# Switched attention in a fused eight-stage kernel: the context product over whole rows and one unit later, with the work of ScalarE, VectorE and GpSimd re-ordered around it

## The chip, the cores and the metric

One NeuronCore of one Trainium2 chip. The metric is the device time of one execution in microseconds (us); lower is better. The kernel before takes 3280.29 us (median of three runs, 3280.03 to 3283.74).

## What is computed

Eight residual sublayers, one after another, on x of shape 128 x 64 x 128: four attention or retention sublayers over a context and four feed-forward ones. The last one, `_L3_ffn_ref`, is the one that the change touches, "switched" attention. Cut to what matters:

```python
gate_v = _get_sel_gate(x, sel_v_w, rs)
gate_o = _get_sel_gate(x, sel_o_w, rs)
q = jnp.einsum('bsd,hpd->bhsp', x, q_w.reshape(H, P, D))
k = jnp.einsum('bsd,hpd->bhsp', x, k_w.reshape(H, P, D))
xv = jnp.einsum('bsd,hedp->bshep', x, v_w.reshape(H, E, D, P))
v = jnp.einsum('bshep,bshe->bhsp', xv, gate_v)
att = jax.nn.softmax(jnp.einsum('bhqp,bhkp->bhqk', q, k) * SCALE, axis=-1)
ctx = jnp.einsum('bhqk,bhkp->bqhp', att, v)
weighted = ctx[:, :, :, None, :] * gate_o[..., None]
out = jnp.einsum('bshep,hepd->bsd', weighted, o_w.reshape(H, E, P, D))
```

There are 8 heads, 8 experts per head, and P = D = 128. `_get_sel_gate` takes a sigmoid of the routing logits, keeps the best two of each head's eight experts, scales them to sum 1 and returns zeros for the others. The input x of the sublayer is first normalised (layer norm), and the result is added to x with a gate.

## The kernel before, in words

The function `switch_attention` is the last stage of the program. It works on 64 tiles. A tile is two batch elements of 64 rows, so 128 rows lie on the 128 partitions. All weights stay in SBUF, each split into a high and a low part, so that one product of high precision is three TensorE passes (high x high, low x high, high x low).

Per tile there are 16 **units**: eight value units v0 to v7 and eight output units o0 to o7, one for each head. A unit (`unit`, L2173) is six matmuls of 512 columns: three into a PSUM bank `ps_sw_a` for experts 4 to 7, then three into a bank `ps_sw_d` for experts 0 to 3. ScalarE empties the first bank (`scale`, L1914): four activations that multiply each expert's block by its gate and write it to `sw_scaled`. VectorE empties the second (`mix`, L2069): two steps of two `scalar_tensor_tensor` that multiply by the gate and accumulate in `sw_v_part` or `sw_o_part`. GpSimd adds up what both left (`add_v`, L1841 and L1846; `add_o`, L1860 to L1870; `finish`). There are two banks of each kind, so a unit may write its banks only when ScalarE and VectorE have emptied those of the unit two before.

Between the units stand the small steps of the tile. On TensorE: `turn_x` (transpose of the normalised x), `turn_probs`, `logits`, two `pair_keys` (L2206, products of 128 x 128, 4 in each), `scores` (L2230) and `context` (L2219, probabilities x values). On ScalarE: copies out of PSUM (`keep_x`, `keep_probs` L1931, `keep_u`, `keep_ctx` L1954) and four steps `exp_scores` (L1963), each the exponential of two heads with a read of the accumulated sum. On VectorE: 20 routing steps R0 to R19 (`route`, from `sw_r_plus` L2078 to `sw_gate_v` L2099), three parts of the layer norm's moments (`front`: `sw_stats`, `sw_mv`, `sw_var`), the normalisation itself (`norm`, `sw_xhat` L244), the row maxima of the scores (`peak`, L2124), the shift derived from them (`shifts`, L2130), the sums of the softmax, and the low parts of the context (`low_ctx`, L2118). On GpSimd: `rstd` (L236), a power of one column.

The order of the work is written out by hand: one list of (lag, step) for each engine, and `straight` issues, for every turn t and every entry in the order of the list, that step for tile t - lag. Each engine executes its list strictly in that order; semaphores tie the engines together. So in one turn TensorE works on the value units of tile t-2, the output units of tile t-3, the scores of tile t-1 and the context of tile t-2. The exponentials of tile t-1 (`exp_scores`) wait for `sw_shift` of the same turn. The text calls a stretch from one v0 to the next "a turn".

The context before is one product for each head and each batch element, on half of the rows:

```python
for h in range(SH):
    for b in range(2):
        t = slice(b * S, (b + 1) * S)
        m = pe.matmul(ps_w[b][:, h * S:(h + 1) * S], v[t, h], probs_T[t, h], start=True, stop=True)
```

Of the kernel before, what the change touches and what calls it, by code (L numbers as in the profile page):

```python
# [1682 lines left out]
def switch_attention(k, A, C, x_in, out):  # L1683
# [6 lines left out]
    with k.scope():  # L1690
# [84 lines left out]
        with nc.Block() as block:  # L1775
# [211 lines left out]
            def _(dve):  # L1987
                dve.memset(zeros[:], 0.0).then_inc(q["zeros"], 1)
                dve.wait_ge(q["zeros"], 1)
# [83 lines left out]
                def route(n):  # L2073


                    def step(i, s, rd):
# [4 lines left out]
                            lambda: dve.tensor_tensor(r["eq1"][:], r["p"][:], wide(rm["m1"][:]), ALU.is_equal),  # L2081
                            lambda: dve.tensor_tensor(r["w1"][:], r["eq1"][:], place[:], ALU.mult),
                            lambda: dve.tensor_reduce(rm["w1"][:], r["w1"][:], AX.X, ALU.max),
                            lambda: dve.tensor_tensor(r["sel1"][:], r["w1"][:], wide(rm["w1"][:]), ALU.is_equal),
# [210 lines left out]
```

## Time and profile before

| what | value |
|---|---|
| median of three runs | 3280.29 us (3280.03 to 3283.74) |
| the profiled execution: its own time | 3283.84 us |
| its span in the profile | 3282.1 us, 78570 instructions |
| TensorE matmuls busy | 2945.8 us (90%) |
| VectorE busy | 2780.9 us (85%) |
| ScalarE busy | 2342.4 us (71%) |
| GpSimd busy | 2319.9 us (71%) |
| chain that ended last | TensorE 57%, of it `ps_sw_a` L2173 23%, `ps_sw_d` L2173 21%, the context L2219 4% |

The span is cut by the profile page into 40 equal slices. The last 23 or so, from about 1400 us on, are the switched attention; there TensorE's digit is 9 (8 in the last slice) and the granted TensorE clock is 9 as well. The stages before it are not touched by the change. In a timeline row, the numbers are start and duration in us, then engine, line, operation and tiles; a value in brackets at its end is the idle time of that engine before it, with what released it. Consecutive instructions of ScalarE and VectorE overlap in their durations, so what one of them costs its engine is the distance to the next start.

### The profile page before, as it was taken

What the parts mean: (1) busy time and instruction counts of PE and PEld (TensorE: products, weight loads), DVE (VectorE), ACT (ScalarE), POOL (GpSimd) and SP (SyncE); (2) the same over time, 40 slices, a digit from 0 to 9 for tenths busy, and PEclk for the clock granted to TensorE, in tenths of its full rate; (3) what the DMA queues carried; (4) which work ended last, traced back from release to release, by engine and by line L of the source; (5) the groups of instructions that cost most, each with busy time, mean ns of one, the idle gap of its engine ahead of it and who ended that gap; (6) DMA issues with size and microseconds to landing.
All of it is one profiled execution on the core that took longest, in us unless ns stands there. A gap on an engine that the chain in (4) does not pass through costs nothing.

```text
span 3282.1 us, 78570 instructions
## 1 busy us (share of the span) xinstructions
PE 2945.8 (90%) x24633; PEld 2215.6 (68%) x24646; DVE 2780.9 (85%) x9101; ACT 2342.4 (71%) x7540; POOL 2319.9 (71%) x3111
## 2 busy tenths in 40 slices
PE   6639998289667999599999999999999999999998
PEld 5526775167435777477777777777777777777776
DVE  4369997599898998698898989898999889898987
ACT  3275665878796666477777777777777777777776
POOL 1179997565687666377777777777777777777777
PEclk7559998589678999799999999999999999999999
DMA  3000000022000110300000000000000000000000
GB/s 107 19 10 17 16 17 8 17 74 72 5 1 17 29 31 28 114 21 8 7 9 9 7 8 8 9 8 8 7 9 9 8 7 9 9 8 8 8 8 5
DMA packets 133086, 63.73 MB, mean 19 GB/s; under 512 B 20544, under 2 KB 132288, under 8 KB 132672
## 3 DMA queue, kind: packets, MB, share of 16 engines
q1 hardware_dynamic: 132672, 58.70, 6.3%
q8 instruction: 200, 3.28, 0.4%
q14 instruction: 214, 1.75, 0.2%
HBM read 41.82 MB, written 8.45 MB: 15 GB/s over the span
## 4 chain that ended last, share of the span: by engine, by line
PE 57%; ACT 1%; DVE 1%; POOL 0%; DMA 0%; issue 0%; SPq 0%; POOLq 0%; ACTq 0%; DVEq 0%
PE ps_sw_a L2173 23%; PE ps_sw_d L2173 21%; PE ps_sw_w L2219 4%; PE ps_sw_w L2206 3%; PE ps_sw_s L2188 2%; PE ps_sw_s L2230 2%; PE ps_sw_m L2195 1%; ACT sw_scaled L1914 0%; PE ps_sw_m L2181 0%; DVE sw_v_part L2069 0%; DMA sw_v<-in_L_ffn_v_w 0%; ACT sw_probs L1963 0%; DVE sw_v_low L2008 0%; ACT sw_v_high L1969 0%; PE ps_sw_w L2236 0%
## 5 line engine op out<-in xcount | busy, mean ns | idle before, releaser
L1914 ACT ACTIVATE sw_scaled<-ps_sw_a,sw_gate_o 128x128 f32<-128x128 f32 x2048 | 620.3, 447 | 254.1 <-PE ps_sw_a L2173 248.2
L1914 ACT ACTIVATE sw_scaled<-ps_sw_a,sw_gate_v 128x128 f32<-128x128 f32 x2048 | 597.4, 448 | 194.4 <-PE ps_sw_a L2173 192.7
L2069 DVE SCALAR_TENSOR_TENSOR sw_o_part<-ps_sw_d,sw_gate_o,sw_o_part 128x128 f32<-128x128 f32 x1920 | 554.9, 338 | 63.2 <-PE ps_sw_d L2173 60.5
L1841 POOL TENSOR_TENSOR sw_v_pair<-sw_v_part,sw_scaled 128x256 f32<-128x256 f32 x512 | 382.1, 746 | 156.0 <-DVE sw_v_part L2069 98.9
L2069 DVE SCALAR_TENSOR_TENSOR sw_v_part<-ps_sw_d,sw_gate_v,sw_scaled 128x128 f32<-128x128 f32 x1024 | 303.7, 337 | 122.1 <-PE ps_sw_d L2173 104.7
L1867 POOL TENSOR_TENSOR sw_o_rest<-sw_o_rest,sw_scaled 128x256 f32<-128x256 f32 x384 | 285.4, 743 | 157.9 <-ACT sw_scaled L1914 120.8
L2069 DVE SCALAR_TENSOR_TENSOR sw_v_part<-ps_sw_d,sw_gate_v,sw_v_part 128x128 f32<-128x128 f32 x1024 | 304.1, 337 | 0.0
L1870 POOL TENSOR_TENSOR sw_o_rest<-sw_o_rest,sw_scaled 128x256 f32<-128x256 f32 x384 | 282.6, 736 | 30.1
L1846 POOL TENSOR_TENSOR sw_v<-sw_v_pair 128x128 f32<-128x128 f32 x512 | 243.8, 476 | 40.1
L985 POOL TENSOR_TENSOR at_key_wide<-at_keyT,c_half_heads 128x1024 f32<-128x1024 f32 x128 | 242.6, 1895 | 4.2 <-ACT at_keyT L1082 4.2
L2173 PE MATMUL ps_sw_a<-sw_v_high,sw_xT_high 128*128 128x512 f32 x512 | 234.6, 458 | 8.2 <-DVE sw_v_low L2008 8.2
L2173 PE MATMUL ps_sw_a<-sw_o_high,sw_ctx_high 128*128 128x512 f32 x512 | 215.7, 421 | 0.5 <-ACT sw_scaled L1914 0.5
L2173 PE MATMUL ps_sw_d<-sw_v_high,sw_xT_high 128*128 128x512 f32 x512 | 207.2, 405 | 0.4 <-DVE sw_v_part L2069 0.4
L2173 PE MATMUL ps_sw_d<-sw_o_high,sw_ctx_high 128*128 128x512 f32 x512 | 202.2, 395 | 1.2 <-DVE sw_v_part L2069 1.2
L2173 PE MATMUL ps_sw_a<-sw_o_high,sw_ctx_low 128*128 128x512 f32 x512 | 203.0, 396 | 0.0
L2173 PE MATMUL ps_sw_d<-sw_o_low,sw_ctx_high 128*128 128x512 f32 x512 | 202.7, 396 | 0.0
L2173 PE MATMUL ps_sw_a<-sw_v_high,sw_xT_low 128*128 128x512 f32 x512 | 202.4, 395 | 0.0
L2173 PE MATMUL ps_sw_d<-sw_o_high,sw_ctx_low 128*128 128x512 f32 x512 | 202.2, 395 | 0.0
L2173 PE MATMUL ps_sw_a<-sw_o_low,sw_ctx_high 128*128 128x512 f32 x512 | 202.1, 395 | 0.0
L2173 PE MATMUL ps_sw_a<-sw_v_low,sw_xT_high 128*128 128x512 f32 x512 | 201.9, 394 | 0.0
L2173 PE MATMUL ps_sw_d<-sw_v_high,sw_xT_low 128*128 128x512 f32 x512 | 201.5, 394 | 0.0
L2173 PE MATMUL ps_sw_d<-sw_v_low,sw_xT_high 128*128 128x512 f32 x512 | 200.7, 392 | 0.0
(337 smaller groups left out, 8584.4 us busy)
## 6 DMA issues: line engine op xcount, KB each, us to landing
at_ctxT<-ctx_T SPq DMA_DIRECT2D x128, 64.0 KB, 1.8
re_values<-in_ctx SPq DMA_DIRECT2D x128, 64.0 KB, 2.4
x<-in_x SPq DMA_DIRECT2D x16, 256.0 KB, 3.4
l_ctx<-in_ctx SPq DMA_DIRECT2D x16, 256.0 KB, 3.0
re_ctx<-in_ctx SPq DMA_DIRECT2D x16, 256.0 KB, 3.2
scratch_x<-x SPq DMA_DIRECT2D x64, 64.0 KB, 1.9
sw_x<-scratch_x SPq DMA_DIRECT2D x64, 64.0 KB, 1.9
sw_x_res<-scratch_x SPq DMA_DIRECT2D x64, 64.0 KB, 1.8
```

Of the source, the lines that this page charges most:

```text
L985: pool.tensor_tensor(key_wide[:, s], keyT[:, s].unsqueeze(1).broadcast_to([P, HALF, P]), C["half_heads"][:].unsqueeze(2).broadcast_to([P, ...
L1841: pool.tensor_tensor(v_pair[:, h % 2], v_part[:, h], scaled[:, h % 4, 2:4], ALU.add)\
L1846: pool.tensor_tensor(v[:, h], v_pair[:, h % 2, 0], v_pair[:, h % 2, 1], ALU.add).then_inc(q["v"], 1)
L1867: pool.tensor_tensor(o_rest[:, 0:2], o_rest[:, 0:2], scaled[:, h % 4, 0:2], ALU.add)\
L1870: pool.tensor_tensor(o_rest[:, 2:4], o_rest[:, 2:4], scaled[:, h % 4, 2:4], ALU.add)\
L1914: act.activation(scaled[:, h % 4, e], ps_a[h % 2][:, e], ACT.Copy, scale=gates[:, s, h, HALF_E + e:HALF_E + e + 1]).then_inc(a_scaled[kind ...
L2069: dve.scalar_tensor_tensor(out=acc[:, e % 2], in0=ps_d[h % 2][:, e], scalar=gates[:, s, h, e:e + 1], in1=before, op0=ALU.mult, op1=ALU.add ...
L2173: m = pe.matmul(bank, lhs[a], w[b][:, h, experts], start=c == 0, stop=c == 2)
L2188: m = pe.matmul(ps_s[t, h], probs[t, s, h], C["ident"][t, t], start=True, stop=True)
L2206: m = pe.matmul(ps_w[n][:, h * P:(h + 1) * P], W["pair"][:, 4 * n + h], xT[:, s], start=True, stop=True)
L2219: m = pe.matmul(ps_w[b][:, h * S:(h + 1) * S], v[t, h], probs_T[t, h], start=True, stop=True)
L2230: m = pe.matmul(ps_s[t], xT[:, s, t], uT[:, :, t], start=True, stop=True)
```

## The change

Five things change, all in `switch_attention`:

- **Context.** `probs_T` becomes 128 x 8 x 128 with zeros outside two diagonal blocks of 64 x 64, cleared once by a memset. `keep_probs` writes the two blocks with two activations instead of one. `context` is then one product of 128 x 128 for each head (8 instead of 16), and it stands behind o2 instead of o1. PSUM bank 0 holds heads 0 to 3, bank 1 heads 4 to 7, each finished separately.
- **ScalarE's list.** Before, after o2: ctx 0, o3, exp 0, o4, ctx 1, o5, exp 1, o6, exp 2, o7, exp 3. Now, after o2: exp 0, exp 1, o3, ctx 0, o4, ctx 1, exp 2, o5, exp 3, o6, o7.
- **VectorE's list.** The norm moves from the head of the value half (for tile t-1) to the middle of the output half (for tile t, behind o2). The three `front` steps move from the output half to the value half. The first `low_ctx` comes one unit later; the second keeps its place. R19 moves one unit ahead.
- **GpSimd's list.** `rstd` moves from between o5 and o6 to directly behind the value units.
- **Scratch.** The tiles `eq1`/`eq2` and `w1`/`w2` of the routing are merged.

```diff
-        probs_T = k.sb("sw_probs_T", [P, SH, S])
+        probs_T = k.sb("sw_probs_T", [P, SH, P])
...
-                stages += [(3, add_o(h)) for h in range(6)] + [(0, rstd)] + [(3, add_o(h)) for h in range(6, SH)]
+                stages += [(0, rstd)] + [(3, add_o(h)) for h in range(SH)]
...
-                    act.activation(probs_T[:], ps_s, ACT.Copy).then_inc(q["p_kept"], 1)
+                    for b in range(2):
+                        t = slice(b * S, (b + 1) * S)
+                        act.activation(probs_T[t, :, t], ps_s[t], ACT.Copy).then_inc(q["p_kept"], 1)
...
-                stages += [(1, keep_u(0)), vs[6], (1, keep_u(1)), vs[7]] + os[:3] + [(2, keep_ctx(0)), os[3], exps[0]]
-                stages += [os[4], (2, keep_ctx(1)), os[5], exps[1], os[6], exps[2], os[7], exps[3]]
+                stages += [(1, keep_u(0)), vs[6], (1, keep_u(1)), vs[7]] + os[:3] + [exps[0], exps[1], os[3], (2, keep_ctx(0))]
+                stages += [os[4], (2, keep_ctx(1)), exps[2], os[5], exps[3], os[6], os[7]]
...
+                dve.memset(probs_T[:], 0.0).then_inc(q["zeros"], 1)
...
-                    "v": [[], [], [(2, sums(0))], [(2, sums(1))], [(2, sums(2))], [], *R[0:5], R[5] + R[6], R[7],
-                          R[8] + R[9], R[10], R[11]],
-                    "o": [R[12], R[13] + R[14], R[15] + R[16], [(1, peak)], [(1, shifts)], R[17], R[18],
-                          [(2, low_ctx(0))], [(0, front(0))], R[19] + [(0, front(1))], [(0, front(2))],
-                          [(2, low_ctx(1))], [], [], [], []],
+                    "v": [[], [], [(2, sums(0))], [(2, sums(1))], [(2, sums(2))], [(0, front(0))], *R[0:4],
+                          R[4] + [(0, front(1))], R[5] + R[6], R[7] + [(0, front(2))], R[8] + R[9], R[10], R[11]],
+                    "o": [R[12], R[13] + R[14], R[15] + R[16], [(1, peak)], [(1, shifts)], [(0, norm)] + R[17], R[18], R[19],
+                          [], [(2, low_ctx(0))], [], [(2, low_ctx(1))], [], [], [], []],
                 }
-                stages = [(1, norm), (1, only_first(keep_pairs))]
+                stages = [(1, only_first(keep_pairs))]
...
                     for h in range(SH):
-                        for b in range(2):
-                            t = slice(b * S, (b + 1) * S)
-                            m = pe.matmul(ps_w[b][:, h * S:(h + 1) * S], v[t, h], probs_T[t, h], start=True, stop=True)
-                            if h == SH - 1:
-                                m.then_inc(q["ctx"], 1)
+                        m = pe.matmul(ps_w[h // 4][:, h % 4 * P:(h % 4 + 1) * P], v[:, h], probs_T[:, h], start=True, stop=True)
+                        if h % 4 == 3:
+                            m.then_inc(q["ctx"], 1)
...
-                stages += [vs[5], (1, pair_keys(1)), vs[6], vs[7], os[0], (1, scores), os[1], (2, context)]
-                stages += os[2:]
+                stages += [vs[5], (1, pair_keys(1)), vs[6], vs[7], os[0], (1, scores), *os[1:3], (2, context)]
+                stages += os[3:]
```

How the lists come out on two engines. ScalarE in the output half of one turn, from the three `scale` steps of o0 to o2 on (x12), before:

```order
L1914 ACTIVATE sw_scaled<-ps_sw_a,sw_gate_o 128x128 x12
L1954 ACTIVATE sw_ctx_high<-ps_sw_w 128x8x64
L1914 ACTIVATE sw_scaled<-ps_sw_a,sw_gate_o 128x128 x4
L1963 ACTIVATE sw_probs,sw_total<-ps_sw_s,sw_shift 128x64 x2
L1914 ACTIVATE sw_scaled<-ps_sw_a,sw_gate_o 128x128 x4
L1954 ACTIVATE sw_ctx_high<-ps_sw_w 128x8x64
L1914 ACTIVATE sw_scaled<-ps_sw_a,sw_gate_o 128x128 x4
L1963 ACTIVATE sw_probs,sw_total<-ps_sw_s,sw_shift 128x64 x2
L1914 ACTIVATE sw_scaled<-ps_sw_a,sw_gate_o 128x128 x4
L1963 ACTIVATE sw_probs,sw_total<-ps_sw_s,sw_shift 128x64 x2
L1914 ACTIVATE sw_scaled<-ps_sw_a,sw_gate_o 128x128 x4
L1963 ACTIVATE sw_probs,sw_total<-ps_sw_s,sw_shift 128x64 x2
```

and now:

```order
L1914 ACTIVATE sw_scaled<-ps_sw_a,sw_gate_o 128x128 x12
L1967 ACTIVATE sw_probs,sw_total<-ps_sw_s,sw_shift 128x64 x4
L1914 ACTIVATE sw_scaled<-ps_sw_a,sw_gate_o 128x128 x4
L1958 ACTIVATE sw_ctx_high<-ps_sw_w 128x512
L1914 ACTIVATE sw_scaled<-ps_sw_a,sw_gate_o 128x128 x4
L1958 ACTIVATE sw_ctx_high<-ps_sw_w 128x512
L1967 ACTIVATE sw_probs,sw_total<-ps_sw_s,sw_shift 128x64 x2
L1914 ACTIVATE sw_scaled<-ps_sw_a,sw_gate_o 128x128 x4
L1967 ACTIVATE sw_probs,sw_total<-ps_sw_s,sw_shift 128x64 x2
L1914 ACTIVATE sw_scaled<-ps_sw_a,sw_gate_o 128x128 x8
```

The exponentials of four heads (x4) now stand ahead of o3, and all eight heads' stand ahead of o6.

VectorE around the shift, from the second mix of o1 on, before:

```order
L2069 SCALAR_TENSOR_TENSOR sw_o_part<-ps_sw_d,sw_gate_o,sw_o_part 128x128 x2
L2124 TENSOR_REDUCE sw_top<-ps_sw_s 128x8
L2069 SCALAR_TENSOR_TENSOR sw_o_part<-ps_sw_d,sw_gate_o,sw_o_part 128x128 x2
L2130 TENSOR_SCALAR sw_shift<-sw_top 128x8
L2069 SCALAR_TENSOR_TENSOR sw_o_part<-ps_sw_d,sw_gate_o,sw_o_part 128x128 x2
L2096 RECIPROCAL sw_m_inv<-sw_m_clip 128x16
```

and now:

```order
L2074 SCALAR_TENSOR_TENSOR sw_o_part<-ps_sw_d,sw_gate_o,sw_o_part 128x128 x2
L2131 TENSOR_REDUCE sw_top<-ps_sw_s 128x8
L2074 SCALAR_TENSOR_TENSOR sw_o_part<-ps_sw_d,sw_gate_o,sw_o_part 128x128 x2
L2137 TENSOR_SCALAR sw_shift<-sw_top 128x8
L2074 SCALAR_TENSOR_TENSOR sw_o_part<-ps_sw_d,sw_gate_o,sw_o_part 128x128 x2
L244 TENSOR_SCALAR sw_xhat<-sw_x,sw_mv,sw_rstd 128x128
L2101 RECIPROCAL sw_m_inv<-sw_m_clip 128x16
```

The maxima and the shift keep their places in VectorE's list; the norm (L244) comes in behind them.

## Rows read from the trace of the kernel before

**Rows 1.** Stretches: length, busy us of PE, PEld, DVE, ACT, POOL, then granted clock, DMA share, GB/s.
```profile
2000.00:2400.00 400.00, 400.00 (x2471) 306.68 (x2470) 359.85 (x1285) 303.66 (x1184) 303.68 (x470) 1.00 0.03 8
```
**Rows 2.** One line's instructions, 1420 to 3200 us: duration ns min/median/max, first and last start us.
```profile
L2124 DVE TENSOR_REDUCE sw_top<-ps_sw_s x60: 676/678/682, 1447.3 to 3194.7; 128x8 f32<-128x512 f32 x60
L2094 DVE TENSOR_TENSOR sw_m_sum<-sw_m_m x60: 268/490/511, 1446.2 to 3193.6; 128x16 f32<-128x16 f32 x60
```
**Rows 3.** Timeline of TensorE over one turn.
```profile
2432.99 0.47 PE L2173 MATMUL ps_sw_a<-sw_v_high,sw_xT_high 128*128 128x512 f32 x1
...
2433.76 0.48 PE L2173 MATMUL ps_sw_d<-sw_v_high,sw_xT_high 128*128 128x512 f32 x1
...
2442.07 1.05 PE L2206 MATMUL ps_sw_w<-sw_xT,sw_pair 128*128 128x128 f32 x8
2442.88 0.48 PE L2173 MATMUL ps_sw_a<-sw_v_high,sw_xT_high 128*128 128x512 f32 x1
...
2450.48 0.50 PE L2173 MATMUL ps_sw_a<-sw_o_high,sw_ctx_high 128*128 128x512 f32 x1
...
2452.07 2.00 PE L2219 MATMUL ps_sw_w<-sw_probs_T,sw_v 64*128 64x64 f32 x32
2454.00 0.50 PE L2173 MATMUL ps_sw_a<-sw_o_high,sw_ctx_high 128*128 128x512 f32 x1
...
2455.51 0.40 PE L2173 MATMUL ps_sw_a<-sw_o_high,sw_ctx_high 128*128 128x512 f32 x1
...
2462.57 0.47 PE L2173 MATMUL ps_sw_a<-sw_v_high,sw_xT_high 128*128 128x512 f32 x1
```
**Rows 4.** Timeline of VectorE in the same turn.
```profile
2446.19 0.80 DVE L2084 TENSOR_TENSOR sw_r_sel<-sw_r_w,sw_m_w 128x128 f32<-128x128 f32 x1
...
2451.98 0.27 DVE L2092 TENSOR_TENSOR sw_r_sel<-sw_r_sel 128x128 f32<-128x128 f32 x1
...
2453.01 0.49 DVE L2094 TENSOR_TENSOR sw_m_sum<-sw_m_m 128x16 f32<-128x16 f32 x1
...
2454.14 0.68 DVE L2124 TENSOR_REDUCE sw_top<-ps_sw_s 128x8 f32<-128x512 f32 x1
2455.71 0.61 DVE L2069 SCALAR_TENSOR_TENSOR sw_o_part<-ps_sw_d,sw_gate_o,sw_o_part 128x128 f32<-128x128 f32 x2 [0.89 <-PE ps_sw_d L2173]
2456.23 0.16 DVE L2130 TENSOR_SCALAR sw_shift<-sw_top 128x8 f32<-128x8 f32 x1
...
2460.39 0.17 DVE L220 BATCH_NORM_AGGREGATE sw_mv<-sw_stats 128x2 f32<-128x6 f32 x1
2460.49 0.57 DVE L2069 SCALAR_TENSOR_TENSOR sw_o_part<-ps_sw_d,sw_gate_o,sw_o_part 128x128 f32<-128x128 f32 x2
```
**Rows 5.** Timeline of VectorE at the stage's start, before GpSimd's adds begin.
```profile
1347.15 0.29 DVE L2084 TENSOR_TENSOR sw_r_sel<-sw_r_w,sw_m_w 128x128 f32<-128x128 f32 x1
```
**Rows 6.** Timeline of ScalarE in the same turn.
```profile
2443.86 1.14 ACT L1914 ACTIVATE sw_scaled<-ps_sw_a,sw_gate_v 128x128 f32<-128x128 f32 x4 [0.82 <-PE ps_sw_a L2173]
...
2455.01 1.14 ACT L1914 ACTIVATE sw_scaled<-ps_sw_a,sw_gate_o 128x128 f32<-128x128 f32 x4 [2.40 <-PE ps_sw_a L2173]
2456.02 0.61 ACT L1954 ACTIVATE sw_ctx_high<-ps_sw_w 128x512 fp32r<-128x512 f32 x1
2456.50 1.17 ACT L1914 ACTIVATE sw_scaled<-ps_sw_a,sw_gate_o 128x128 f32<-128x128 f32 x4
2457.50 0.37 ACT L1963 ACTIVATE sw_probs<-ps_sw_s,sw_shift 128x64 f32<-128x64 f32 x1
...
2458.07 1.21 ACT L1914 ACTIVATE sw_scaled<-ps_sw_a,sw_gate_o 128x128 f32<-128x128 f32 x4
...
2461.12 1.31 ACT L1914 ACTIVATE sw_scaled<-ps_sw_a,sw_gate_o 128x128 f32<-128x128 f32 x4
```
**Rows 7.** Timeline of GpSimd in the same turn.
```profile
2451.46 0.46 POOL L1846 TENSOR_TENSOR sw_v<-sw_v_pair 128x128 f32<-128x128 f32 x1
2452.74 0.73 POOL L1860 TENSOR_TENSOR sw_o_rest<-sw_scaled 128x256 f32<-128x256 f32 x1 [0.82 <-issue]
...
2462.87 0.55 POOL L236 TENSOR_TENSOR sw_rstd<-sw_var,minus_half 128x1 f32<-128x1 f32 x1
```

More of the change, by code:

```diff
@@ L1725, in switch_attention @@
         decays = k.sb("sw_exp", G)
-        r = {n: k.sb("sw_r_" + n, G) for n in ("plus", "p", "eq1", "w1", "sel1", "p2", "eq2", "w2", "sel2", "sel")}
+        r = {n: k.sb("sw_r_" + n, G) for n in ("plus", "p", "eq", "w", "sel1", "p2", "sel2", "sel")}
         rm = {n: k.sb("sw_m_" + n, [P, 2 * SH]) for n in ("m1", "w1", "m2", "w2", "sum", "clip", "inv")}
@@ L1928, in keep_probs @@
                     act.wait_ge(q["p_turned"], 2 * i + 2)
-                    if not first(i, 1):
+                    if i == 0:
+                        act.wait_ge(q["zeros"], 2)
+                    else:
                         act.wait_ge(q["ctx"], 2 * i)
-                    act.activation(probs_T[:], ps_s, ACT.Copy).then_inc(q["p_kept"], 1)
+                    for b in range(2):
+                        t = slice(b * S, (b + 1) * S)
+                        act.activation(probs_T[t, :, t], ps_s[t], ACT.Copy).then_inc(q["p_kept"], 1)
                 def exp_logits(i, s, rd):
@@ L1953, in step @@
                             act.wait_ge(d_made["o"], SH * (i - 1))
-                        act.activation(ctx_high[:, s, :, b], ps_w[b].rearrange("p (h t) -> p h t", h=SH), ACT.Copy)\
+                        act.activation(ctx_high[:, s, 4 * b:4 * b + 4].rearrange("p h b t -> p (h b t)"), ps_w[b], ACT.Copy)\
                             .then_inc(q["ctx_high"], 1)
@@ L2080, in step @@
                             lambda: dve.tensor_reduce(rm["m1"][:], r["p"][:], AX.X, ALU.max),
[L2081 to L2084, printed above, removed]
+                            lambda: dve.tensor_tensor(r["eq"][:], r["p"][:], wide(rm["m1"][:]), ALU.is_equal),
+                            lambda: dve.tensor_tensor(r["w"][:], r["eq"][:], place[:], ALU.mult),
+                            lambda: dve.tensor_reduce(rm["w1"][:], r["w"][:], AX.X, ALU.max),
+                            lambda: dve.tensor_tensor(r["sel1"][:], r["w"][:], wide(rm["w1"][:]), ALU.is_equal),
                             lambda: dve.scalar_tensor_tensor(out=r["p2"][:], in0=r["sel1"][:], scalar=-2.0, in1=r["p"][:],
@@ L2117, in step @@
                         dve.wait_ge(q["ctx_high"], 2 * i + b + 1)
-                        dve.tensor_tensor(ctx_low[:, s, :, b], ps_w[b].rearrange("p (h t) -> p h t", h=SH),
-                                          ctx_high[:, s, :, b].bitcast(F32), ALU.subtract).then_inc(q["ctx_low"], 1)
+                        half = slice(4 * b, 4 * b + 4)
+                        dve.tensor_tensor(ctx_low[:, s, half].rearrange("p h b t -> p (h b t)"), ps_w[b],
+                                          ctx_high[:, s, half].rearrange("p h b t -> p (h b t)").bitcast(F32), ALU.subtract)\
+                            .then_inc(q["ctx_low"], 1)
                     return step
@@ L2225, in scores @@
                     if not first(i, 1):
-                        waits.append((q["p_kept"], i))
+                        waits.append((q["p_kept"], 2 * i))
                     wait_alone(pe, *waits)
```

12 lines of the change are left out of this document (6 added, 6 removed).

## The prediction

> **What bounds the kernel now.** Read first how busy the engines are in a steady stretch of the stage: in 400 us TensorE is busy for 400.00, VectorE for 359.85, ScalarE for 303.66 and GpSimd for 303.68, at the full granted clock [rows 1]. So TensorE is the bound, and VectorE has about a tenth to spare. Next the length of a turn: 60 row maxima start between 1447.3 and 3194.7 us, which makes 1747.4 / 59 = 29.62 us per turn [rows 2]; the turn that I walk through takes 2462.57 - 2432.99 = 29.58 us [rows 3]. All times below count from its first matmul of v0 (2432.99).
>
> Then the timelines, to see where each engine waits. VectorE waits for TensorE only once in the output half, 0.89 us, because TensorE is in the context product [rows 4]; ScalarE waits 2.40 us there [rows 6]. From 2456 us on ScalarE has no idle time left: copy of the context, o3, exponentials, o4 and so on follow each other up to the next v0. Its `scale` of o6 starts at 2461.12 and lasts 1.31, so it ends at 2462.43 [rows 6], and v0, which needs that bank, starts at 2462.57 [rows 3]. In its output half ScalarE is thus just on time. That is what the prediction turns on.
>
> **TensorE's own part.** The context of 32 records takes 2454.00 - 2452.07 = 1.93 us [rows 3]. Now it is 16 records of 128 x 128; the nearest row is `pair_keys`, 8 such records in 2442.88 - 2442.07 = 0.81 us [rows 3], so 1.62 us and a gain of 0.31 us. Bounds: 0 to 0.5. Start to start, a record of a half takes 1.93 / 32 = 0.060 and a full one 0.101 us, so two halves cost 0.12. The Trainium skill, "TensorE: Matmul & The Clock Gate", Part 3, says that small-K matmuls on distinct row groups of the array run concurrently; by that two halves would cost no more than one full product, and the gain would be nothing or a loss. No row here shows such an overlap in full, and the measured difference stands.
>
> v0 and v1 lose about 0.08 us each at one of their banks because they wait for the old owner (0.48 instead of 0.40 us [rows 3]); I give back 0.16. TensorE alone would then need: o1 at 2450.48, which is 17.49, less 0.16, is 17.33; o1 takes 1.51 (as the unit behind an insertion does, 2454.00 to 2455.51), o2 1.41 (a fifth of 2455.51 to 2462.57), the gap ahead of the context 0.1, the context 1.62, o3 1.51, o4 to o7 4 x 1.41 [rows 3]. Sum 29.1 us: 0.47 less per turn, if nothing else is late.
>
> **What is late next: the exponentials.** ScalarE's list now has exp 0 and exp 1 directly behind o2 and ahead of o3, and both wait for the shift. The shift's place in VectorE's list is unchanged. Its maxima start at 2454.14; the mix behind it waited 0.89 us and could have started at 2454.82; the mix costs 0.52 (2455.71 to 2456.23) [rows 4]. So without TensorE's context in the way the shift starts at 2455.34, which is 22.35. Before it in the chain two `front` steps are now added: one costs 0.10 (2460.39 to 2460.49) [rows 4], the other I take alike, 0.20 together; the third falls into a wait of the value half. TensorE's 0.16 comes off, because the chain hangs on v3. The shift then starts at 22.39 and is there 0.16 later [rows 4], at 22.55. The norm comes behind it and costs this chain nothing.
>
> Now ScalarE, in order: four exponential steps of 0.57 (2457.50 to 2458.07) are 2.28; `scale` of o3, o4, o5, o6 at 1.00 each (2456.50 to 2457.50) are 4.00; two context copies of 0.48 (2456.02 to 2456.50) are 0.96 [rows 6]. That is 7.24 to the start of what follows o6. The last `scale` ends 0.31 behind that point (1.31 against 1.00), and v0 started 0.14 behind its end [rows 3, 6]. Sum: 22.55 + 7.24 + 0.45 = 30.24 us from v0 to v0. Before, ScalarE had only exp 0 and exp 1 ahead of o6, and it had copied the context and done o3 before it needed the shift; now 1.14 us more of exponentials lie ahead of o6, and some 1.7 us of waiting for the shift behind o2. **The period becomes 30.24 - 29.58 = 0.66 us longer,** and TensorE's gain of 0.31 vanishes in its wait at o7 and v0.
>
> **The other edits.** The second activation of `keep_probs` costs another 0.48 (as a copy of 512 columns) on ScalarE ahead of v4; the wait of 0.82 us before v5 covers it [rows 6]. Without that cover 0.48 would be added to the scaling of v5. The norm leaves the head of the value half, where VectorE waits for TensorE afterwards: nothing. Later `low_ctx` is needed only by the next turn: nothing. The memset at the start stands ahead of weights that are still loading: under 1 us. Merged scratch adds no wait, since its users were already in order. `rstd` (0.55 us) now runs directly behind the last value add (2451.46 + 0.46), and R13 starts at 2451.98 beside it [rows 4, 7]. No row shows a VectorE step beside `rstd`; R15 beside an add takes 0.49 us where its shortest is 0.27 [rows 2, 4], and R6 takes 0.80 where it took 0.29 with GpSimd quiet [rows 4, 5]. So R13 may end up to 0.35 later; but R15 at 2453.01 was held until about 2453.5 by the add that started at 2452.74 [rows 7], so most of that falls into a wait that is there already. I take 0, with 0 and 0.67 as bounds (the upper one is a rival below).
>
> **Sum.** 64 tiles, of which some 60 turns are full: 60 x 0.66 = +40 us on the profiled execution's 3283.84 us (span 3282.1), 3324 us. It lies 3.6 us above the median of the runs, so against that median I predict **3321 us**.
>
> **Rivals.**
>
> 1. *More blocking behind GpSimd.* R13 waits for `rstd`, and GpSimd's first output add (2452.74 before; ready at about 2452.6 now) starts ahead of R14, so that R14 waits out 0.73 us and R15 meets the second add. R14 then ends near 2453.45, the mix near 2453.97, R15 near 2454.2, against 2453.54: 0.67 later. The shift and all behind it move along: 1.33 us per turn, +80 us, 3360 us. For it: the waits of 0.49 and 0.80 us [rows 4]. Against it: R13 and R14 were free, and VectorE may come first. By the rule of the Trainium skill, "SBUF — State Buffer", Who interferes with whom, a VectorE instruction with two SBUF inputs and a GpSimd instruction that reads SBUF exclude each other for the whole instruction, also for one column; R13 is then surely held, and this rival hangs on R14 alone. The trace agrees for the adds (0.49 against 0.27 us).
>
> 2. *Faster: the shift comes in time and TensorE stays the bound.* Then a turn is 29.1 us, -0.47 x 60 = -28 us, 3252 us. The point from which it decides: 30.24 falls to 29.58 if the shift starts at 21.73 instead of 22.39, and to 29.1 at 21.25. For it: on the way to the shift VectorE loses about 0.5 us in R6, as much in its twin R9, and 0.2 in R15 to GpSimd [rows 2, 4, 5]; with `rstd` out of the output half GpSimd is earlier, and two of these waits gone would do. Against it: R6 is held by an add that VectorE's own mix has just released, so it moves along. A small part of this would give no change: 0.66 saved, 3280 us.
>
> 3. *The rest of ScalarE runs faster than I take it:* the exponentials at 0.5 instead of 0.57, less tail. Some 0.3 us per turn remain, +18 us, 3298 us. Against it: the row's distance repeats at each step.
>
> **How the numbers follow.** My forecast, with its bounds of about 0.35 to 1.0 us per turn, 0.57; rival 1, 0.18; rival 2 in full or in large part, 0.12; its partial form, no change, 0.05; rival 3, 0.08. A change of under 0.2% (6.6 us) can't be told from none. Faster by more than that 0.12, within it 0.05, slower 0.83. The range leaves out rival 2 and no change (0.17): 3297 to 3362 us.
>
> **What the profile after would show.** TensorE's busy share in the steady stretch falls from 100% to some 97 or 98%, with waits of its weight loads for ScalarE's `scale` in front of o7 and v0. The context is one group of 16 records over about 1.6 us. ScalarE waits 1.5 us or more for the shift at its first exponential, and not at all from there to o6. The row maxima come 30.2 to 30.3 us apart. The forecast is wrong if ScalarE finds the shift ready at the first exponential, or if TensorE still shows 400 of 400 us busy. If the maxima are 30.9 us apart and R14 lasts 0.7 us or more, rival 1 holds.

## The result, and the profile after

The changed kernel takes **3309.23 us** (median of 4 runs, 3301.71 to 3316.69); the kernel before, run beside it, takes 3282.01 us (4 runs, 3280.03 to 3284.41). The ratio is 1.0085, with a 95% interval from 1.0068 to 1.0101: it is slower by 0.85%. The prediction of 3321 us (3297 to 3362) had the sign, the place and the mechanism; the rise is 27 us where 40 were forecast.

The profiled execution of after took 3316.69 us, with a span of 3314.6 us. Its page answers to the numbers shown of before (busy shares, and the chain that ended last):

```profile
span 3314.6 us, 76601 instructions
...
PE 2950.3 (89%) x23622; PEld 2210.0 (67%) x23622; DVE 2766.1 (83%) x9102; ACT 2410.6 (73%) x7604; POOL 2325.6 (70%) x3111
...
DVE 24%; PE 18%; ACT 11%; issue 6%; POOL 0%; DMA 0%; DVEq 0%; ACTq 0%; SPq 0%; POOLq 0%
```

TensorE is nearly as busy as before over the whole program, but its share of the chain that ended last has fallen from 57% to 18%. VectorE (24%) and ScalarE (11%) now hold more of the chain than TensorE. The steady stretch says the same; this row answers to [rows 1]:

```profile
2000.00:2400.00 400.00, 393.31 (x2234) 300.17 (x2233) 347.91 (x1256) 312.58 (x1178) 302.57 (x468) 1.00 0.03 8
```

TensorE was busy for 400.00 of 400 us and is busy for 393.31 (98.3%). The granted clock is 1.00 of full speed in both, that is 2.4 GHz, so the clock has no part in the result. The row maxima, one per turn, answer to [rows 2]:

```profile
L2131 DVE TENSOR_REDUCE sw_top<-ps_sw_s x59: 677/680/682, 1477.6 to 3227.1; 128x8 f32<-128x512 f32 x59
```

(3227.1 - 1477.6) / 58 = 30.16 us per turn against 29.62. That is +0.55 us, 33 us over 60 turns, and the two profiled executions differ by just that: 3316.69 - 3283.84 = 32.85 us. So the loss lies in the turn.

Where in the turn? The waits of after, 1450 to 3250 us (total us, times, longest):

```profile
ACT sw_scaled L1914 <- PE ps_sw_a L2179: 284.8, 358, 1.7
...
ACT sw_probs L1967 <- DVE sw_shift L2137: 85.6, 59, 1.5
PEld ps_sw_a L2179 <- ACT sw_scaled L1914: 80.6, 180, 0.9
...
PE ps_sw_a L2179 <- ACT sw_scaled L1914: 27.2, 60, 0.5
```

Row two is new: 59 times, 1.45 us each, ScalarE stands still for the shift. Rows three and four are what comes of it: TensorE's weight loads, three times in each turn (ahead of o5, o6 and o7), and then its matmuls, ahead of o7, wait for a `scale` of ScalarE. The timelines show how the one leads to the other. VectorE first, with v0 at 2391.47 (all "from v0" numbers below count from there):

```profile
2410.69 0.28 DVE L2097 TENSOR_TENSOR sw_r_sel<-sw_r_sel 128x128 f32<-128x128 f32 x1
2411.00 0.29 DVE L2098 TENSOR_TENSOR sw_chosen<-sw_r_p,sw_r_sel 128x128 f32<-128x128 f32 x1
...
2411.73 0.22 DVE L2099 TENSOR_TENSOR sw_m_sum<-sw_m_m 128x16 f32<-128x16 f32 x1
...
2412.59 0.68 DVE L2131 TENSOR_REDUCE sw_top<-ps_sw_s 128x8 f32<-128x512 f32 x1
2413.18 0.60 DVE L2074 SCALAR_TENSOR_TENSOR sw_o_part<-ps_sw_d,sw_gate_o,sw_o_part 128x128 f32<-128x128 f32 x2
2413.70 0.16 DVE L2137 TENSOR_SCALAR sw_shift<-sw_top 128x8 f32<-128x8 f32 x1
```

The 0.89 us of waiting that stood ahead of the mix before [rows 4] is gone, since TensorE no longer does the context at that point. The shift starts at 22.23 from v0. Then ScalarE:

```profile
2399.71 1.21 ACT L1935 ACTIVATE sw_probs_T<-ps_sw_s 64x512 f32<-64x512 f32 x2
2400.95 2.38 ACT L1914 ACTIVATE sw_scaled<-ps_sw_a,sw_gate_v 128x128 f32<-128x128 f32 x8
...
2411.30 1.14 ACT L1914 ACTIVATE sw_scaled<-ps_sw_a,sw_gate_o 128x128 f32<-128x128 f32 x4 [0.25 <-PE ps_sw_a L2179]
2413.90 0.32 ACT L1967 ACTIVATE sw_probs<-ps_sw_s,sw_shift 128x64 f32<-128x64 f32 x1 [1.45 <-DVE sw_shift L2137]
...
2415.07 1.16 ACT L1914 ACTIVATE sw_scaled<-ps_sw_a,sw_gate_o 128x128 f32<-128x128 f32 x4
2416.07 0.65 ACT L1958 ACTIVATE sw_ctx_high<-ps_sw_w 128x512 fp32r<-128x512 f32 x1
...
2420.18 2.34 ACT L1914 ACTIVATE sw_scaled<-ps_sw_a,sw_gate_o 128x128 f32<-128x128 f32 x8
```

After the wait of 1.45 us there is no bracket any more down to o6 at 2420.18: 6.28 us in which ScalarE never stops. That is the list working off what it missed; o3's `scale` starts at 2415.07, 1.57 us behind the first matmul of o3 (2413.50 below). TensorE and its weight loads (the rows marked PEld) at the end of the turn:

```profile
2411.80 1.95 PE L2223 MATMUL ps_sw_w<-sw_probs_T,sw_v 128*128 128x128 f32 x16
2413.50 0.48 PE L2179 MATMUL ps_sw_a<-sw_o_high,sw_ctx_high 128*128 128x512 f32 x1
...
2419.91 0.50 PE L2179 MATMUL ps_sw_a<-sw_o_high,sw_ctx_high 128*128 128x512 f32 x1 [0.46 <-ACT sw_scaled L1914]
...
2421.63 0.47 PE L2179 MATMUL ps_sw_a<-sw_v_high,sw_xT_high 128*128 128x512 f32 x1
```

```profile
2419.91 0.19 PEld L2179 LDWEIGHTS ps_sw_a<-sw_o_high,sw_ctx_high 128*128 128x128 f32 x1 [0.89 <-ACT sw_scaled L1914]
...
2421.60 0.19 PEld L2179 LDWEIGHTS ps_sw_a<-sw_v_high,sw_xT_high 128*128 128x128 f32 x1 [0.46 <-issue]
```

o7 needs the bank that o5's `scale` empties, and its weight load waits 0.89 us; v0 needs the bank of o6, and its weight load waits 0.46 us again. The second wait has the label "issue", that is, no releaser that the profile shows. ScalarE's row names the likely one: o6's `scale` starts at 2420.18 and, with the 1.31 us that it takes in the kernel before [rows 6], ends near 2421.5. In x9 and x10 below, where ScalarE is early, that wait of v0 is gone. From v0 to v0 the turn is 2421.63 - 2391.47 = 30.16 us.

### The profile page after: what moved, and what is told of

It reads as the page before. It is cut to its first block, busy times and chain, and to the rows that moved or that the text cites. A ratio compares the mean times of both kernels' runs of the same rounds, so it can differ in the third digit from the quotient of the medians.

```text
span 3314.6 us, 76601 instructions
## 1 busy us (share of the span) xinstructions
PE 2950.3 (89%) x23622; PEld 2210.0 (67%) x23622; DVE 2766.1 (83%) x9102; ACT 2410.6 (73%) x7604; POOL 2325.6 (70%) x3111
## 4 chain that ended last, share of the span: by engine, by line
DVE 24%; PE 18%; ACT 11%; issue 6%; POOL 0%; DMA 0%; DVEq 0%; ACTq 0%; SPq 0%; POOLq 0%
DVE sw_v_part L2074 10%; PE ps_sw_a L2179 8%; ACT sw_scaled L1914 6%; PE ps_sw_d L2179 6%; DVE sw_o_part L2074 5%; ACT sw_probs L1967 3%; PE ps_sw_s L2194 2%; ACT sw_ctx_high L1958 2%; DVE sw_r_p L2084 1%; DVE sw_r_plus L2083 1%; PE ps_sw_m L2201 1%; DVE sw_r_sel L2096 1%; DVE sw_r_w L2087 1%; DVE sw_r_sel L2089 1%; DVE sw_r_eq L2086 1%
## 5 line engine op out<-in xcount | busy, mean ns | idle before, releaser
L1914 ACT ACTIVATE sw_scaled<-ps_sw_a,sw_gate_v 128x128 f32<-128x128 f32 x2048 | 587.5, 375 | 200.5 <-PE ps_sw_a L2179 186.1
L1914 ACT ACTIVATE sw_scaled<-ps_sw_a,sw_gate_o 128x128 f32<-128x128 f32 x2048 | 599.8, 440 | 123.9 <-PE ps_sw_a L2179 117.5
L2179 PE MATMUL ps_sw_a<-sw_o_high,sw_ctx_high 128*128 128x512 f32 x512 | 226.7, 443 | 28.1 <-ACT sw_scaled L1914 28.1
L1967 ACT ACTIVATE sw_probs<-ps_sw_s,sw_shift 128x64 f32<-128x64 f32 x512 | 170.2, 374 | 101.8 <-DVE sw_shift L2137 101.8
```

Source lines behind the costliest of these rows:

```text
L1914: act.activation(scaled[:, h % 4, e], ps_a[h % 2][:, e], ACT.Copy, scale=gates[:, s, h, HALF_E + e:HALF_E + e + 1]).then_inc(a_scaled[kind ...
L1967: act.activation(probs[:, s, h], ps_s[:, h], ACT.Exp, bias=shift[:, s, h:h + 1], scale=float(P) ** -0.5, accum_out=total[:, s, h:h + 1]).t ...
L2179: m = pe.matmul(bank, lhs[a], w[b][:, h, experts], start=c == 0, stop=c == 2)
```

## The experiments

The theory: a turn is as long as the chain of shift, four exponential steps, two context copies, four `scale` steps and v0 makes it in ScalarE's new order, and the other edits cost or gain little. The rivals: VectorE held by GpSimd ahead of the shift makes the loss; or the context behind o2 does; or the moved norm and `front` do. Ratios are to the kernel before, run in the same session (medians 3282.66 us for the first four, 3280.10 for the next four, 3284.43 for the last two). "Per turn" is the spacing of the row maxima from 1480 to 3200 us.

**x1_after_again:** the changed kernel itself, as the base of the others.

> The changed kernel once more, beside the three edits of it that follow, so that they share the runs of the kernel before. Both theories: 1.0068 to 1.0101 of the kernel before, as the first comparison had it (about 3309 us), and row maxima 30.16 us apart (29.62 before).

3311.08 us, ratio 1.0098 (1.0082 to 1.0113); 30.16 us per turn. The same turn as in the first measurement; the turn is the steadier measure, since the place in time at which the stage begins differs by some us from run to run (the first of all row maxima starts at 1349.5 us in the first profile, at 1344.4 in this one).

**x2_exp_order_old:** after, with ScalarE's output half in the order of before. Nothing else. (In this diff and the one under x10 each line is a part of a `stages +=` line, and the third pair under x10 is the start of a line.)

```diff
-    os[:3] + [exps[0], exps[1], os[3], (2, keep_ctx(0))]
-    [os[4], (2, keep_ctx(1)), exps[2], os[5], exps[3], os[6], os[7]]
+    os[:3] + [(2, keep_ctx(0)), os[3], exps[0]]
+    [os[4], (2, keep_ctx(1)), os[5], exps[1], os[6], exps[2], os[7], exps[3]]
```

> The changed kernel with ScalarE's output half in the order of the kernel before (context copy 0, o3, exponentials 0, o4, context copy 1, o5, exponentials 1, o6, exponentials 2, o7, exponentials 3); all else as changed. Theory (the turn is the chain shift, all exponentials, four scale steps, v0): the chain goes, TensorE is the bound again and keeps the gain of the full-row context: 29.1 to 29.3 us per turn, 3252 to 3262 us, 0.5 to 0.9% faster than before. Rival (the full-row context, its second activation or the moved norm costs the time): it stays at or above 30.0 us per turn, about 3305 us.

3260.85 us, ratio 0.9935 (0.9922 to 0.9947); 29.27 us per turn. With this order undone, the rest of the change wins 0.65% where the whole lost 0.98%: the order of ScalarE's list costs 30.16 - 29.27 = 0.89 us per turn, more than the whole loss of 0.55. This is the decisive run. Its maxima and steady stretch:

```profile
L2131 DVE TENSOR_REDUCE sw_top<-ps_sw_s x59: 674/678/681, 1497.3 to 3195.1; 128x8 f32<-128x512 f32 x59
```

```profile
2000.00:2400.00 400.00, 400.00 (x2292) 311.10 (x2290) 360.64 (x1295) 322.69 (x1224) 310.05 (x480) 1.00 0.03 8
```

In ScalarE's timeline of it, the exponentials follow o3 and find the shift there (it starts at 2405.80), without a bracket:

```profile
2404.99 0.60 ACT L1958 ACTIVATE sw_ctx_high<-ps_sw_w 128x512 fp32r<-128x512 f32 x1 [0.45 <-PE ps_sw_w L2223]
2406.59 1.15 ACT L1914 ACTIVATE sw_scaled<-ps_sw_a,sw_gate_o 128x128 f32<-128x128 f32 x4 [1.00 <-PE ps_sw_a L2179]
2407.61 0.33 ACT L1967 ACTIVATE sw_probs<-ps_sw_s,sw_shift 128x64 f32<-128x64 f32 x1
```

**x6_before_exp_order:** the counterpart, the kernel before with ScalarE's new order alone (the diff above with its signs exchanged).

> The kernel before, with ScalarE's changed order of the output half as the only edit (exponentials 0 and 1 directly behind o2, and so on); context on half rows behind o1. Theory (a turn is the start of the shift, plus 7.93 us as measured in the changed kernel: 30.16 - 22.23): there the shift starts at 23.24 us, since VectorE waits for TensorE's context, so 23.24 + 7.93 = 31.17 us per turn, 1.55 more than before, some +90 us, 3370 us. Rival (the order of ScalarE's list alone is harmless; it costs only together with the moved context): below 30.0 us per turn.

3367.51 us, ratio 1.0260 (1.0237 to 1.0282); 31.02 us per turn. The order by itself costs 1.40 us per turn in the kernel before, more than in after (0.89), because there the context still stands ahead of the shift: the shift starts at 2456.23 - 2432.99 = 23.24 us from v0 [rows 3, 4], and with the 7.93 us that after takes from the shift's start to v0 (30.16 - 22.23) that makes 31.17, as expected, against 31.02 measured. The trace of x6 splits this: from the shift's start (2412.50) to v0 (2420.43) it takes 7.93 us, just as in after, and the missing 0.15 lies ahead of the shift, which starts at 23.09 and not at 23.24 from v0. Its row of the first exponential:

```profile
2412.70 0.32 ACT L1963 ACTIVATE sw_probs<-ps_sw_s,sw_shift 128x64 f32<-128x64 f32 x1 [0.28 <-DVE sw_shift L2130]
```

ScalarE waits only 0.28 us for the shift here, and yet this is the slowest kernel of all. The idle time ahead of the exponential does not tell the cost: before it, ScalarE waited 2.39 us for TensorE's o2, and the work that now lies behind the exponentials was pushed out all the same.

**x3_half_row_context:** after, with the context product back on half rows, behind o2; and **x5_exp_old_half_rows:** the same on top of x2.

```diff
-    for h in range(SH):
-        m = pe.matmul(ps_w[h // 4][:, h % 4 * P:(h % 4 + 1) * P], v[:, h], probs_T[:, h], ...)
+    for h in range(SH):
+        for b in range(2):
+            t = slice(b * S, (b + 1) * S)
+            m = pe.matmul(ps_w[b][:, h * S:(h + 1) * S], v[t, h], probs_T[t, h], ...)
```

> The changed kernel with the context on half rows as before (16 products, both banks finished together), behind o2; the lists of all engines as changed, the two activations of keep_probs kept. Theory: the 0.3 us per turn that the full-row product saves on TensorE lie inside a wait for ScalarE, so nothing changes: 30.1 to 30.3 us per turn, within 4 us of the changed kernel. Rival (TensorE's work counts in the changed kernel): 0.3 us per turn more, some 18 us slower than the changed kernel.

> As x2 (ScalarE's order of the kernel before, all else changed), and the context on half rows again, behind o2. Theory (in x2 TensorE is the bound, so its work counts there in full): 1.93 against 1.62 us for the context, so 0.31 us per turn more than x2's 29.27, 29.58 us per turn, some 19 us slower than x2 and about level with the kernel before. Rival (the full-row product gives nothing there either, since two half-row products run side by side in the array): 29.27 us per turn, as x2.

x3: 3317.88 us, ratio 1.0109 (1.0095 to 1.0123), 30.16 us per turn, that of the changed kernel (30.155, in x1 30.159). Its median lies 6.8 us above that of x1, where 4 us at most were expected, but the two intervals overlap and the turn is the same. So in after the full-row product gains nothing. x5: 3284.56 us, ratio 1.0011 (1.0000 to 1.0022), 29.62 us per turn against 29.27 of x2. With ScalarE out of the way the full-row product is worth 0.35 us per turn, 21 us over 60 turns (the ratios differ by 0.0076, 25 us). The same edit is worth 0 or 0.35, and which it is depends on another engine. The product itself, in x5 and in x2:

```profile
2417.09 0.39 PE L2177 MATMUL ps_sw_d<-sw_o_high,sw_ctx_low 128*128 128x512 f32 x1
2417.41 2.00 PE L2223 MATMUL ps_sw_w<-sw_probs_T,sw_v 64*128 64x64 f32 x32
2419.34 0.50 PE L2177 MATMUL ps_sw_a<-sw_o_high,sw_ctx_high 128*128 128x512 f32 x1
```

```profile
2403.67 0.40 PE L2179 MATMUL ps_sw_d<-sw_o_high,sw_ctx_low 128*128 128x512 f32 x1
2403.90 1.95 PE L2223 MATMUL ps_sw_w<-sw_probs_T,sw_v 128*128 128x128 f32 x16
2405.61 0.48 PE L2179 MATMUL ps_sw_a<-sw_o_high,sw_ctx_high 128*128 128x512 f32 x1
```

1.93 us for the half rows (2417.41 to 2419.34), 1.71 for the full ones: 0.22 of the 0.35. Another 0.09 stands ahead of the product: the first half-row product starts 0.32 us behind the last matmul of o2 (2417.09 to 2417.41), the first full-row one 0.23 (2403.67 to 2403.90), as one matmul of a unit behind another does. This leaves some 0.04 us that was not followed up.

**x4_maxima_early:** after, with the maxima and the shift two places earlier in VectorE's list, so that ScalarE's new order finds the shift there.

```diff
-    "o": [R[12], R[13] + R[14], R[15] + R[16], [(1, peak)], [(1, shifts)], [(0, norm)] + R[17], R[18], R[19],
+    "o": [R[12], [(1, peak)], [(1, shifts)] + R[13] + R[14], R[15] + R[16], [], [(0, norm)] + R[17], R[18], R[19],
```

> The changed kernel with the row maxima and the shift earlier in VectorE's list: the maxima behind the second mix of o0, the shift behind the first mix of o1, R13 and R14 behind the shift; ScalarE's list as changed. Theory: the shift is there about 2 us earlier, before ScalarE is done with o2, so its wait of 1.45 us at the first exponential is gone; ScalarE then waits for TensorE at o3, from where its list (two context copies, exponentials 2 and 3 and the scales of o3 to o6) is still a little longer than TensorE's five units: 29.6 to 29.95 us per turn, 3280 to 3302 us, faster than the changed kernel and not faster than before. Rival (the wait for the shift costs nothing, or VectorE's later mixes of o1 hold TensorE): 30.1 us per turn or more, 3309 us or slower.

3272.45 us (9 runs), ratio 0.9973 (0.9962 to 0.9983); 29.57 us per turn. It is better by 0.59 us than after, the wait for the shift is gone, and it is slightly faster than before. That missed the range on record (29.6 to 29.95 us per turn, 3280 us or more) on the fast side. ScalarE's rows of it, around o3:

```profile
2420.29 0.35 ACT L1967 ACTIVATE sw_probs<-ps_sw_s,sw_shift 128x64 f32<-128x64 f32 x1
...
2421.59 1.15 ACT L1914 ACTIVATE sw_scaled<-ps_sw_a,sw_gate_o 128x128 f32<-128x128 f32 x4 [0.86 <-PE ps_sw_a L2179]
```

The first two exponential steps are done early, and ScalarE then waits 0.86 us for TensorE's o3. o3's `scale` starts 0.98 us behind o3's first matmul (at 2420.61) and not 1.57 as in after: that is the 0.59. From there to v0 both kernels take the same 6.56 us (2421.59 to 2428.15; 2415.07 to 2421.63). So of the 0.89 us between after and x2, 0.59 is o3's `scale` held by the late shift. The other 0.30 stays in x4: from o3 on, ScalarE's list with two context copies and exponential steps 2 and 3 ahead of o6 is still longer than TensorE's work, and the shift has no more part in it.

**x7_lists_old:** after, with VectorE's and GpSimd's lists of before: norm, `front`, `low_ctx`, R19 and `rstd` back in their places, ScalarE's new order kept.

> The changed kernel with VectorE's and GpSimd's lists of the kernel before (norm at the head of the value half, the three front steps in the output half, low_ctx 0 one unit earlier, rstd between o5 and o6); context and ScalarE's order as changed. Theory (the moved norm and rstd do not lie on the way to the shift, which comes by some 0.2 us earlier without the two front steps, and by some 0.1 to 0.3 without the longer wait of R0): 29.7 to 30.1 us per turn, 0 to 0.4 less than the changed kernel. Rival (those lists are what slows the changed kernel, the exponentials not): 29.3 us per turn.

3311.67 us, ratio 1.0091 (1.0072 to 1.0109); 30.07 us per turn. All those moves together cost 0.09 us per turn in after, by the spacing of the maxima; the times cannot tell x7 from x1.

**x8_context_alone:** the kernel before with the full-row context behind o2 and its two activations, its memset and the merged scratch; the lists of ScalarE, VectorE and GpSimd are those of before.

> The kernel before with the full-row context behind o2 and its two activations as the only edits; the lists of ScalarE's exponentials, VectorE and GpSimd as before. Theory (the context is the part of the change that gains, and the others neither help nor harm TensorE while ScalarE is in time): 29.2 to 29.4 us per turn, within 0.15 us of x2, about 3260 us. Rival (the moved norm and front steps are needed for the gain): 29.6 us per turn, as before.

3251.89 us, ratio 0.9912 (0.9892 to 0.9931); 29.18 us per turn. It differs from x2 by the lists of VectorE and GpSimd alone, and by the same 0.09 us (29.27). So of the five edits the context is the gain, ScalarE's order the loss, and the two other lists cost a little. The context gains 29.62 - 29.18 = 0.44 us per turn, of which the full rows are 0.35 (x5 against x2); the other 0.09 would then be its place behind o2, which was not tried alone. Nor was the merged scratch, which is in x8 too.

**x9_maxima_early_list and x10_context_maxima_early:** can the two be joined? x9 is x4 with three exponential steps ahead of o6 instead of four, and the first two around the context copy. x10 has the same two orders on top of x8; the diff is x10's against x8.

```diff
-    os[:3] + [(2, keep_ctx(0)), os[3], exps[0]]
-    [os[4], (2, keep_ctx(1)), os[5], exps[1], os[6], exps[2], os[7], exps[3]]
+    os[:3] + [exps[0], (2, keep_ctx(0)), exps[1], os[3]]
+    [os[4], (2, keep_ctx(1)), os[5], exps[2], os[6], os[7], exps[3]]
...
-    "o": [R[12], R[13] + R[14], R[15] + R[16], [(1, peak)], [(1, shifts)], R[17], R[18],
+    "o": [R[12], [(1, peak)], [(1, shifts)] + R[13] + R[14], R[15] + R[16], [], R[17], R[18],
```

> After with VectorE's maxima and shift taken earlier (as in x4_maxima_early) and with ScalarE's list exp 0, context copy 0, exp 1, o3, o4, context copy 1, o5, exp 2, o6, o7, exp 3, so that only three of the four exponential steps lie ahead of o6. My theory: the chain from the shift through ScalarE to v0 was what held x4 at 29.57 us per turn (its maxima 29.572 apart, TensorE 399 of 400 us busy); one exponential step of 0.57 less in it leaves TensorE as the bound, at about 29.1 to 29.2 us per turn, 3247 to 3256 us, TensorE busy for 400 of 400 us. Rival: x4's remaining loss against x8 (29.18) comes from VectorE's changed order and not from ScalarE; then the turn stays at 29.4 to 29.6 us, 3265 us or more.

> x8_context_alone (before with the full-row context behind o2 and its two activations) plus the maxima and the shift earlier on VectorE and ScalarE's list of x9. If TensorE is the bound in x8 (29.18 us per turn), an earlier shift buys nothing: 29.15 to 29.2 us, 3248 to 3256 us. If part of x8's turn still waits for the shift or for ScalarE, it falls below 29.1 us, 3245 us or less. If VectorE's R13 and R14 now come too late for the routing, it is slower than x8 by 0.1 us per turn or more.

x9: 3240.47 us, ratio 0.9875 (0.9856 to 0.9893), 29.00 us per turn, below the 29.1 to 29.2 that I had expected. The turn is 0.57 us shorter than x4's, which is also the length of one exponential step, but that is chance: behind o3 the new list has one step and one context copy less ahead of o6 (1.05 us), and what stops the gain at 0.57 is TensorE, busy for 400 of 400 us. The theory on record for x9, that the chain from the shift held x4, was wrong too, as x4's wait for o3 shows. x10: **3235.84 us**, ratio 0.9863 (0.9843 to 0.9883), 28.97 us per turn, faster than before by 1.4% and the fastest of all. Of the three cases in its expectation it is the second: part of x8's turn did still wait for ScalarE. The row of x8's waits that shows it, 1480 to 3200 us:

```profile
PEld ps_sw_a L2180 <- ACT sw_scaled L1914: 19.9, 59, 0.4
```

The same row of x10's waits:

```profile
PEld ps_sw_a L2180 <- ACT sw_scaled L1914: 0.5, 1, 0.5
```

And x10's maxima, for the length of its turn:

```profile
L2131 DVE TENSOR_REDUCE sw_top<-ps_sw_s x59: 669/673/675, 1495.1 to 3175.5; 128x8 f32<-128x512 f32 x59
```

In x8 a weight load waits 19.9 / 59 = 0.34 us for ScalarE in every turn; in x10 it does so once in 59 turns, and a turn is 0.21 us shorter. Which of x10's two new orders does it was not tried singly.

## Why the prediction was right, point by point

**The bound.** "ScalarE is just on time", read from a `scale` that ended 0.14 us ahead of v0 [rows 3, 6], was the point on which everything turned, and x2 and x6 show it from both sides. The forecast of 3321 us lies 12 us above the measured 3309; the sum 3280.29 + 60 x 0.66 makes 3320, so 1 us of that is rounding. What I read from the 400.00 busy us [rows 1], that TensorE alone is the bound, was not quite right: x8, x2 and x10 all show 400.00 of 400 and take 29.18, 29.27 and 28.97 us per turn.

**TensorE's own part.** The context was put at 1.62 us and takes 1.70 (2411.80 to 2413.50), so the gain in the product is 0.23 and not 0.31: a record of it takes 0.106 us start to start, where I had 0.101 from `pair_keys`. Against that, the 0.1 us that I kept as a gap ahead of the context is not there (0.23 us from the last matmul of o2, as between any two matmuls of a unit), so the two errors nearly cancel. TensorE alone was put at 29.1 us per turn; x9 and x10, where it hardly waits, take 29.00 and 28.97. That this gain vanishes in waits at o7 and v0 is what the rows show, and x3 shows it by taking the gain away: the turn does not change. By the rule of the Trainium skill, "TensorE: Matmul & The Clock Gate", Part 3, the two half products would have cost no more than a full one; x5 against x2 does not agree (1.93 against 1.71 us, and 0.35 us per turn). A half-row record of 64 columns takes 0.060 us start to start, more than half of the 0.107 of a full one with 128 columns, so nothing in these rows shows two halves side by side.

**The chain.** Term by term, predicted and measured:

| term | predicted | measured |
|---|---|---|
| start of the shift, from v0 | 22.39 | 22.23 |
| to the first exponential | 0.16 | 0.20 |
| from there to o6's `scale`: four exponential steps, o3 to o5, two copies | 6.24 | 6.28 |
| o6's `scale` to v0 | 1.45 | 1.45 |
| turn | 30.24 | 30.16 |

The shift was put 0.16 too late, and the two terms behind it 0.08 too short. Of the 0.16, 0.09 is a mistake: the maxima were counted with their full 0.68 us, but the mix starts 0.59 us behind them (2412.59 to 2413.18), as consecutive VectorE steps overlap. That the rest is only 0.07 is luck. I had taken the steps that run beside GpSimd's adds as unchanged, and they changed in both directions: to the next start, R15 now costs 0.25 us where it cost 0.53 and R3 0.20 instead of 0.42, but R0 costs 0.50 instead of 0.15 and R4 0.32 instead of 0.22; the two `front` steps cost 0.15 instead of 0.20. Against the spacing of the maxima before (29.62) the rise is 0.55 instead of 0.66 us, 33 us instead of 40. The other 6 us between the forecast and the measured rise of 27 us lie between the runs: the profiled execution of after, against which the sum holds (3324 predicted, 3316.69 measured), is the slowest of its four.

**Costs taken as nothing.** The second activation of `keep_probs` was put at 0.48 us more. The two together take 1.24 us to the next start (2399.71 to 2400.95); 0.76 us more than the 0.48 of a copy before. The wait of 0.82 us ahead of v5 [rows 6] just covered that too: the eight `scale` activations behind them (2400.95) show no wait any more. Norm, `low_ctx` and `rstd` were put at nothing and the two `front` steps at 0.20 on the way to the shift; with R19 they cost 0.09 us per turn together (x7; x8 against x2).

**Rival 1** (more blocking behind GpSimd, 30.9 us) needed R13 held by `rstd` and R14 by an add. Neither is held; for R14 the case did not arise, since the add begins only at 2411.18, with R14 under way. The durations of all turns, min/median/max ns:

```profile
L2097 DVE TENSOR_TENSOR sw_r_sel<-sw_r_sel x59: 274/276/277, 1475.7 to 3225.2; 128x128 f32<-128x128 f32 x59
L2098 DVE TENSOR_TENSOR sw_chosen<-sw_r_p,sw_r_sel x59: 291/293/295, 1476.0 to 3225.5; 128x128 f32<-128x128 f32 x59
L2099 DVE TENSOR_TENSOR sw_m_sum<-sw_m_m x59: 220/221/227, 1476.7 to 3226.2; 128x16 f32<-128x16 f32 x59
```

**Rival 2** (the shift in time, TensorE the bound, 29.1 us) did not happen in after, since the shift came at 22.23 and not before 21.73. Its price was right, but its condition was not. An early shift was said to be enough: 29.1 us from 21.25 on. In x4 the shift starts at 20.31 from v0 (2418.90 - 2398.59), and the turn is still 29.57, no shorter than before, since o3's `scale` cannot start before 23.00, when TensorE's product for it is there, and ScalarE's list takes 6.56 us from there to v0. Only with a shorter list ahead of o6 as well, in x9, is the turn 29.00. **Rival 3** (faster exponentials) fell: two steps take 1.17 us, 0.58 each.

**What the profile after was to show** it shows in the main: weight loads waiting at o7 and at v0, 16 records for the context, no stop from the first exponential to o6. Three numbers are a little off: TensorE 98.3% busy (97 or 98 were said), the maxima 30.16 us apart (30.2 to 30.3), the wait for the shift 1.45 us (1.5 or more).

## What to carry to other kernels

In an engine that works off a list strictly in order, ask of every entry moved forward when its input arrives, and then count what stands behind it up to the next point at which another engine waits. The price is how late that work now is for the other engine, and not the idle time in front of the moved entry (0.28 us of idle time and 1.40 us per turn lost in x6; 1.45 of idle time in after, of which x4 gets back 0.59). Do it also when the engine is busy for only three quarters of the time. And test the edits of a bundle singly: here the context alone was worth 28 us (x8) and ScalarE's order cost 0.89 us per turn, 50 us (x1 against x2).

## What the runs showed of the hardware

- **A one-column GpSimd operation did not hold VectorE.** In after `rstd` runs beside R13, a VectorE step with two SBUF inputs. GpSimd's timeline in the same turn:

```profile
2410.60 0.55 POOL L236 TENSOR_TENSOR sw_rstd<-sw_var,minus_half 128x1 f32<-128x1 f32 x1
2411.18 0.74 POOL L1860 TENSOR_TENSOR sw_o_rest<-sw_scaled 128x256 f32<-128x256 f32 x1
```

R13 starts at 2410.69 and takes 0.28 us, as in every turn (274 to 277 ns above), and as without `rstd` beside it (0.27 [rows 4]). R14, from 2411.00, takes 0.29 beside the end of `rstd`, also as before; an add that is already under way when R14 starts was not put to the test. The Trainium skill, "SBUF — State Buffer", Who interferes with whom, would have `rstd` and R13 exclude each other, since it names no size from which on that holds; this trace does not agree, with the reserve that GpSimd's spans in a profile are rough. It does agree for the adds of 256 columns (R6: 0.80 us, and 0.29 with GpSimd quiet [rows 4, 5]). Which steps they hold changes with the order. R15 went from 490 ns [rows 2] to 221, and R0, with a median of 227 ns before, now takes 575: it starts at 2399.88 beside an add that ends at 2400.38. The medians of R0 and of the norm in after:

```profile
L2083 DVE TENSOR_SCALAR sw_r_plus<-sw_exp x60: 318/575/668, 1464.9 to 3244.5; 128x128 f32<-128x128 f32 x60
L244 DVE TENSOR_SCALAR sw_xhat<-sw_x,sw_mv,sw_rstd x59: 332/338/343, 1479.3 to 3228.8; 128x128 f32<-128x128 f32 x59
```

The norm takes 338 ns in its new place and took 792 in the old one. The 0.45 us shows in no time: with the norm (and the other moves) back in its old place, x7 has the shorter turn.

- **Half the partitions, no less time.** An activation of 64 x 512 takes 593 ns; the one of 128 x 512 that two of them replace took 624 ns in the kernel before (median). One copy of before, and the new ones of after:

```profile
2441.39 0.62 ACT L1931 ACTIVATE sw_probs_T<-ps_sw_s 128x512 f32<-128x512 f32 x1
```

```profile
L1935 ACT ACTIVATE sw_probs_T<-ps_sw_s x120: 592/593/597, 1464.7 to 3244.9; 64x512 f32<-64x512 f32 x120
```

Start to start it is worse: the two take 0.62 us each (2399.71 to 2400.95), the one copy 0.47 (2441.39 to 2441.86), since its end overlapped with the next activation and theirs do not. Splitting by partitions raised ScalarE's cost of `keep_probs` to two and a half times.

- **A product on half the rows costs a gap as well.** The first half-row product of the context starts 0.32 us behind the matmul before it, the first full-row one 0.23 (x5 and x2 above). Why was not tested.

- **400 of 400 us busy is not a proof of a bound.** The ends of matmuls are modelled, and a start that comes 0.1 us late leaves no gap in the record. The waits of the weight loads (19.9 us in x8, 0.5 in x10, with 400.00 us busy in both) showed the 0.2 us per turn that the busy time hid.
